# A graph network on one core: the five gather passes rebuilt on four row slots of 16 batches

## What is computed

```python
h = relu(layernorm(x))                     # before every layer
# layer 0, three times:
agg = segment_sum(h[src], dst, n)
h   = relu(concatenate([h, agg / (count + 1)]) @ W + b)
# layer 1: graph attention over the edges (and loops), then a feed-forward net
# layer 2:
aggr = segment_sum(relu(h[src] + edge_attr), dst, n)
z = (1 + eps) * h + aggr                   # then two matmuls with batch norms
# layer 3:
out = x + h + segment_sum(h[src] + edge_attr, dst, n)
```

## Time and profile before

| | us |
|---|---|
| three runs | 17120.43, 17063.85, 16991.23 (median 17063.85) |
| the profiled execution | 16898.69 |
| its span, first to last instruction | 16896.7 |

### The profile page before, as it was taken

How to read it: one execution, slowest core, us unless ns; L and a number is a source line. 1 busy time by engine, 2 the same in 40 slices (tenths; PEclk the granted TensorE clock), 3 DMA queues, 4 the chain that set the end, 5 groups by cost and what they waited for, 6 DMA issues and landing times. The chain is left out here.

```text
span 16896.7 us, 120575 instructions
## 1 busy us (share of the span) xinstructions
PE 6796.4 (40%) x30243; PEld 5870.2 (35%) x30244; DVE 3299.2 (20%) x6637; ACT 824.4 (5%) x1247; POOL 9578.3 (57%) x9860
## 2 busy tenths in 40 slices
PE   3444443333333444310000009996555555533333
PEld 2434333333333333200000008873555555333333
DVE  3222221111111222100000014444111112311111
ACT  1000000000000000000000000003000000200000
POOL 2666666666666666667777440001666664366666
PEclk8555555555555555555555555557555555655555
DMA  2111111111111222133333212222222222221212
GB/s 85 48 48 48 48 47 46 48 47 49 48 47 53 58 56 57 53 86 100 100 100 99 68 33 82 100 92 82 79 85 83 83 79 90 67 55 53 55 52 53
DMA packets 593156, 1124.64 MB, mean 67 GB/s; under 512 B 220826, under 2 KB 364385, under 8 KB 566579
## 3 DMA queue, kind: packets, MB, share of 16 engines
q0 software_dynamic: 307488, 624.42, 14.6%
q1 hardware_dynamic: 285622, 499.73, 8.8%
HBM read 904.32 MB, written 218.95 MB: 66 GB/s over the span
## 5 line engine op out<-in xcount | busy, mean ns | idle before, releaser
L680 POOL DMA_INDIRECT work<-rows_a,index x4704 | 4544.1, 966 | 2425.0 <-issue 1475.6
L751 PE MATMUL psum<-onehot,work 128*128 128x64 f32 x12544 | 2864.0, 416 | 3649.9 <-issue 1191.6
L680 POOL DMA_INDIRECT work<-rows_b,index x3136 | 3088.4, 985 | 1771.2 <-issue 1039.4
L751 PEld LDWEIGHTS psum<-onehot,work 128*128 128x128 f32 x12544 | 2721.0, 325 | 3797.5 <-issue 2795.1
L1191 POOL DMA_INDIRECT work<-attention_rows,index x1568 | 1608.7, 1026 | 610.6 <-issue 559.1
L751 PE MATMUL psum<-onehot,regionB 128*128 128x64 f32 x6272 | 1550.0, 417 | 720.8 <-issue 564.0
L751 PEld LDWEIGHTS psum<-onehot,regionB 128*128 128x128 f32 x6272 | 1438.7, 327 | 816.6 <-issue 789.8
L846 DVE TENSOR_TENSOR regionA<-regionA,psum 128x64 f32 x2352 | 508.7, 216 | 5116.3 <-remote 3598.3
L765 PE MATMUL psum<-onehot,regionB 128*4 128x64 f32 (+1 forms) x6272 | 1171.4, 358 | 467.2 <-issue 466.5
L765 PEld LDWEIGHTS psum<-onehot,regionB 128*4 128x4 f32 (+1 forms) x6272 | 1021.7, 224 | 516.9 <-issue 470.5
L182 POOL COPY work<-regionB 128x500 f32 (+1 forms) x75 | 45.3, 603 | 2030.6 <-DVE regionB L561 2030.6
(11 more groups left out here) (253 smaller groups left out, 4638.8 us busy)
## 6 DMA issues: line engine op xcount, KB each, us to landing
gathered_rows<-work SPq DMA_DIRECT2D x98, 1088.0 KB
work<-gathered_rows SPq DMA_DIRECT2D x98, 1088.0 KB, 4.9
regionB<-in_edge_attr SPq DMA_DIRECT2D x195, 512.0 KB
work<-rows_a,index POOLq DMA_INDIRECT x4704
work<-rows_b,index POOLq DMA_INDIRECT x3136
work<-attention_rows,index POOLq DMA_INDIRECT x1568
x_transposed<-regionA SPq DMA_DIRECT2D x75, 250.0 KB, 6.0
rows_a<-regionC SPq DMA_DIRECT2D x50, 250.0 KB
```

Of the source, the lines that this page charges most:

```text
L680: pool.indirect_dma_start(rows3[h][:, t, :], None, table, bass.IndirectOffsetOnAxis(ap=net.index[:, k, h * ST + t:h * ST + t + 1], axis=0) ...
L751: last = nc.tensor.matmul(bank_of(h, q, 0), msgs3[h][:, t, 0:D], onehot[:, h * ST + t, :], start=(k == 0), stop=(k == GT - 1))
```

## The change

`aggregate` is split: `attend` keeps the attention pass as it was, `gather_pass` is new and serves agg0, agg1, agg2, agg4 and agg5.
- Four row slots of 16 batches in region `B` (`SLOTS = 4`). The last two halves of the 98 are written out behind the loop of 24 rounds of four slots.
- One PSUM bank per slot. PE waits once per slot for `added` (the adds of the same slot's last use) and raises `summed` once per slot, after 16 batches.
- DVE casts 16 index columns per slot, behind the slot's adds, and raises `staged`; POOL waits for `staged` and `summed[s]`.
- Own features are no longer resident in `B`: n0 and n3 store `h` to HBM (`keep=True`), each chunk's own features are loaded two chunks ahead (`load_own`), and the Sage layers store theirs.
- The follow-up of a chunk runs in two parts: `vector` behind slot 3, `vector_late` and PE's part behind slot 1 of the next round.
- agg4 adds the attributes in place (`rows + attr` in `B`), ACT rectifies in place, attributes lie in `C` in four slots and no longer go through PE. `net.ES` is gone.
- agg5 loads the attributes itself and sums them on PE into the same group, 16 more matmuls per slot. `Finish` no longer loads the stored sum; its loads and stores are issued by ACT.

```diff
@@ gather_pass, was aggregate
-    S = 2 if attention or edges else 4
-    ST, SG = 2 * HALF // S, 2 * GPH // S
-    rows = [net.work[:, h * ST * XW:h * ST * XW + ST * width] for h in range(S)]
+    rows = [net.B[:, s * T:(s + 1) * T] for s in range(SLOTS)]
+    attr = [net.C[:, s * T:(s + 1) * T] for s in range(SLOTS)]
...
+    bank_of = lambda s, q, k=0: net.psum[:, s * 512 + k * GPH * W + q * W:s * 512 + k * GPH * W + (q + 1) * W]
...
+                def gather(j, s):
+                    pool.wait_ge(staged, r * (NHALF + 2) + j * SLOTS + s + 1)
+                    pool.wait_ge(summed[s], use(s, r, j) + 1)
+                    pool.sem_inc(allowed, 1)
+                    for t in range(HALF):
+                        pool.indirect_dma_start(
...
+                def load(j, s):
+                    if edges:
+                        sp.wait_ge(message[s], use(s, r, j) + 1)
+                    else:
+                        sp.wait_ge(summed[s], use(s, r, j) + 1)
...
+                def sums(j, s):
+                    pe.wait_ge(piled[s], built(r, j) + 1)
+                    if edges:
+                        pe.wait_ge(relued[s], use(s, r, j) + 1)
+                    else:
+                        pe.wait_ge(gathered[s], use(s, r, j) * 16 * HALF + 16 * HALF)
+                    if final:
+                        pe.wait_ge(attr_loaded[s], use(s, r, j) * 16 + 16)
+                    pe.wait_ge(added, half(r, j, s) * GPH + GPH)
+                    for q in range(GPH):
+                        for k in range(GT):
+                            t = q * GT + k
+                            last = nc.tensor.matmul(bank_of(s, q), rows3[s][:, t, :], onehot[s][:, t, :],
+                                                    start=(k == 0), stop=(k == GT - 1 and not final))
+                        for k in range(GT if final else 0):
+                            t = q * GT + k
+                            last = nc.tensor.matmul(bank_of(s, q), attr[s][:, t * D:(t + 1) * D], onehot[s][:, t, :],
+                                                    start=False, stop=(k == GT - 1))
...
+                    last.then_inc(summed[s], 1)
+                with pe.Fori(0, PAIRS) as j:
+                    for s in range(SLOTS):
+                        sums(j, s)
+                        if follow and s == 1:
+                            due_range(net, pe, j * 2 - 2, j * 2, lambda c: follow.tensor(pe, c))
...
+            if follow:
+                due_range(net, pe, NIT - 3, NIT - 1, lambda c: follow.tensor(pe, c))
+                due_range(net, pe, NIT - 1, None, lambda c: follow.tensor(pe, c))
...
+                def messages(s, j):
+                    dve.wait_ge(gathered[s], use(s, r, j) * 16 * HALF + 16 * HALF)
+                    dve.wait_ge(attr_loaded[s], use(s, r, j) * 16 + 16)
+                    nc.vector.tensor_tensor(rows[s], rows[s], attr[s], ALU.add).then_inc(message[s], 1)
...
+                with dve.Fori(0, PAIRS) as j:
+                    for s in range(SLOTS):
+                        add(j, s)
+                        n = dve.snap(j * SLOTS + (s + SLOTS))
+                        following = dve.snap(j + 1)
+                        stage(n, s)
+                        compare(n, s, following)
+                        if edges:
+                            messages((s + 2) % SLOTS, j if s < 2 else following)
+                        if follow and s == 1:
+                            due_range(net, dve, j * 2 - 2, j * 2, lambda c: follow.vector_late(dve, c))
+                    if follow:
+                        due_range(net, dve, j * 2, j * 2 + 2, lambda c: follow.vector(dve, c),
+                                  lambda: all_added(half(r, j, SLOTS) * GPH))
...
@@ gin_output
-            sp.dma_start(net.ES, Cc[:, 0:N]).then_inc(s["kept"], 16)
@@ new helper
+def load_own(net, sp, f, c):
+    if not isinstance(c, int):
+        sp.wait_ge(f.own_loaded, c * 16)
+    elif c:
+        sp.wait_ge(f.own_loaded, 16 * c)
+    sp.dma_start(own(net, c), net.HT[:, bass.ds(c * CH, CH)]).then_inc(f.own_loaded, 16)
```

571 lines of the change are left out of this document (314 added, 257 removed).

## The result

The kernel after takes 17,662.44 us (median of four, 17,583.29 to 17,703.93), the kernel before beside it 17,092.14 (16,991.23 to 17,220.62). The ratio is 1.0365, with a 95% interval of 1.0308 to 1.0421: slower by 3.7%, where the forecast was 15,780 and faster. (A ratio given with an interval is that of the executions in the faster state of the program, so it can differ from the quotient of the medians, which is 1.033 here.) The profiled execution took 17,583.29 us, its span is 17,581.1.

A forecast was written before the change was run, and what follows sets the result against it. POOL's indirect gathers bound the kernel, with some 1714 us of pauses from late PE signals. Five passes -1284, with +26 and -17, gave -1275: 15,624 us profiled, 15,780 with 1% carried; range 15,500 to 16,400.

The forecast's parts named there:

- 46 us are left for the signal: Ring of 4 x 16: 80 us until POOL's first slot wait, less 20 filling and 13.5 for landing, PE, adds, cast.
- 210 in all: POOL's pauses after the change: 30 us in agg0, agg1, agg5, 70 in agg2, 50 in agg4; bounds 0 and 1714.
- The term of agg5: Last pass: 16 more batches per slot on PE covered; attribute loads cost 55 ns x 1568 = 86 us.
- the rival to that term: agg5: descriptors wait for DVE, not traffic, so gathers stay at 959 ns, sum 86 us lower; no chance given.
- agg4 gained: Edge pass: four slots, attributes added in place, PE's work per slot halved; 2132 us forecast, -413.
- The tails: Ends of passes: three chunks left after the last gather instead of one; 122 us in Project, 48, 43, 20, 43 elsewhere.
- gin: This stage loses the 6.4 MB store ahead of its loads: about -17 us.
- n0 and n3: These stages now store h too: +13 us each, +26 together.
- the stage sums: Head, gathers, pauses and tail of agg0, agg1, agg2, agg4, agg5: 2081, 2038, 2162, 2132, 2129 us, together -1284.
- D: Gather passes: PE's signals come only when POOL pauses, Project's chain on top; pauses 1737 us, median 17,320; chance 0.04.
- B: Gather passes: POOL still stops 5.5 us once per ring, 135 us per pass, +465, total 16,250; chance 0.20.
- C: agg4 and agg5: traffic slows gathers to 1.383 us per DMA, +116 us each, total 16,010; chance 0.09.

The follow-up runs named there:

- a_attr_by_dve: Changed kernel with the last pass's attributes added to the rows by one VectorE instruction per slot, not 16 matmuls: ratio 1.0129 on chip D, 1.0070 on chip E.
- a_one_add: Changed kernel with VectorE adding a slot's four groups in one instruction at a fixed place, output wrong; about 15,230 us on chip B.
- a_half_one: Changed kernel with half of the sums' matmuls left out and one VectorE add per slot at a fixed place; about 15,280 us on chip B.
- a_third: The changed kernel as it is, run again on chip D: 15,291.95 us beside 15,162.70 for the kernel before.
- b_again: The kernel before, unchanged, profiled on chip C: 17,018 us, beside 17,339 for the changed kernel.

## Why the prediction was wrong

**The step that failed** is "So 46 us are left for the signal, against 25 as the longest seen", and the 30, 70, 50 and 30 us of pauses taken from it, "210 in all: near the lower end, as 25 is well under 46". Pauses came to 2,091 us. The step has two faults.

First, 25 us was neither the longest wait nor the delay. The earlier trace rows leave out agg4, where VectorE's waits in the kernel before reach 41.5 us (TensorE's own sums are a part of them):

```profile
DVE regionC L843 <- remote: 1094.9, 87, 41.5
```

And a wait begins only when VectorE gets there. Counted from the end of a group's last matmul to the start of its add (the ends are modelled, and VectorE's other work is in it), the kernel before has a median of 10.8 us in agg1 and 33.2 at most. The very sums of the earlier trace rows ended at 3026.36 and were added at 3051.85, 25.5 us later, behind a wait of 15.41. Nor do the next matmuls start at 3052.13; this row stands between the two that the earlier trace rows show:

```profile
3033.87 3.98 PE L751 MATMUL psum<-onehot,work 128*128 128x64 f32 x16 [5.80 <-DMA work<-rows_b,index]
```

So the 46 us were not far above what the trace held. In the kernel after the same count gives 58.7 us at most in agg1 and 61.0 in agg0, over the 46, and on chip D 0.7 in agg1.

Second, the step has the matmuls at full pace and only their signal late, by a length that a longer ring outlasts. What the runs showed in its place is that the streams themselves are slow beside the gathers (2.8 us a matmul instruction, 0.70 us a short VectorE one), so that they fall behind for as long as this lasts. "Why, I can't read; that it is late is what counts" was the sentence to stop at: the whole gain rested on how that delay goes with the ring. That the longer ring itself makes the backlog larger fits the longest wait, 20.9 us before and 82.7 after, and is not shown: the ring of 32 on a chip with slow streams is the run that is missing, and agg4 of the kernel before, with a ring of 32 batches, has 145 matmul instructions at 2.8 us where its agg1 has 8.

**The term of agg5** failed by the same cause. "16 more batches per slot on PE (14.6 of 20 us, covered)" is right where no stream is slow: on chip D the pass takes 2058 us with them. Where streams are slow they cost 264 to 301 us. The 86 us that I charged for the attribute traffic aren't there: on chip D agg5 has 982 ns a gather with the traffic and agg1 991 without. The Trainium skill, page SBUF — State Buffer, section "SBUF: two separate sides", by which descriptor writing waits for VectorE and not for traffic, was the rival to that term; these numbers agree with it in sign, and so do the 1034 ns of a_attr_by_dve. Its size doesn't follow from VectorE's work alone: on chip D agg0, with more of it than agg1, has 990 ns against 991, and on chip B agg1 has 974 in a_one_add and 994 in a_half_one, with the same adds.

**What came right.** agg4 gained, by 186 us and not 413: half its matmuls left. The tails are 47, 30, 105, 19 and 70 us against 48, 43, 122, 20 and 43 worked out. gin gave 14 (forecast 17), n0 and n3 15 and 11 (13 each). And where the streams aren't slow the stage sums are near: 2073, 2066, 2115, 2103, 2058 against 2081, 2038, 2162, 2132, 2129. That is in part luck, as terms cancel: in agg1 the gathers take 2031 us and not 1960, the pauses 0 and not 30, the tail 30 and not 43. The whole was forecast at 15,624 for the profiled execution, with gat_gather at 2190; chip D has 1995 there, which makes 15,429, and 15,292 was measured. But on such a chip the kernel before has none of the 1,714 us either, at least by its time: 16,899 less 1,714 less 195 is 14,990, and it takes 15,163. I had no profile of it there, so its stages on such a chip, and with them the 130 us between the two kernels, stay unread.

**The rivals.** D had the right outcome and nearest time (17,320), with half of the mechanism: it had signals come only in POOL's pauses. What happens is that TensorE's and VectorE's own instructions are held up as well. It had .04, and its condition, a delay of over 46 us, was the right one. B's pause per ring (24.5 a pass) is within a factor of two of the count (39, 28, 39, 21 and 47 pauses of over 2 us) and far from the length: 5.5 us priced, 8 to 13 in the median. C falls: the gathers of agg5 take 986 ns, not over 1.05 us.

**Why slower, and not even.** Where streams are slow no pass of any version here took under 2,266 us, so all stayed above the forecast's 2,040 to 2,160. agg5 got 3,136 more matmul instructions on TensorE, +389 to +413 us, which agg4 gives back only with 146 to 186; agg0 and agg1 lost 60 to 90 us each. Of that last piece 25 to 38 us are the longer gathers of agg1 (979 ns against 955 to 963) and 6 to 20 the tail; the rest is longer pauses, and which part of the new order makes them was not settled.

## What to carry to other kernels

Before pricing a stall that the trace doesn't name ("remote", "issue"), ask whether it grows with the load: a delay may be outlasted by a deeper buffer, a backlog is not. Measure a late signal from the end of the work to its use; the waiting engine's own wait shows only a part of it. Take a second profile on a second chip before building on a wait, since here the kernel before took 15,160 us on two of the chips and 17,000 on the others. Where streams of instructions are slow beside indirect DMAs, work moved from many small instructions to one large one gained in one pass (a_attr_by_dve, -264 to -301 us), and where they aren't it lost there (+76). Halving the matmuls of the kernel before gained in one pass of five, so try it before counting on it.

## What the runs showed of the hardware

Beside indirect DMAs the other engines' streams were slow on chips A, C, E and on that of the first profiles: 2.8 us per matmul instruction, 0.70 us per short VectorE instruction, and 1.38 us per gather in gat_gather, with TensorE idle. On chips B and D the same programs showed 1.263 us per gather in gat_gather (1980 us from first to last) and nothing slow.

The slow instructions of both engines keep one step. In agg1 of the kernel after, TensorE's matmuls start 0.70, 1.4, 2.1, 2.8 or 3.5 us behind the one before (67, 49, 73, 201 and 14 of them, to 0.05 us), and VectorE's short instructions last 0.70 or 1.4 us (494 and 23). In the same pass of a_third there are 1 and 6 such matmuls and no such VectorE instruction.

The two kinds of chip differ in one more thing. Here are the gathers in the list of DMA issues (count, then the median us from issue to landing), first of after, then of a_third:

```profile
regionB<-rows_a,index POOLq DMA_INDIRECT x4704
...
work<-attention_rows,index POOLq DMA_INDIRECT x1568
```

```profile
regionB<-rows_a,index POOLq DMA_INDIRECT x4704, 2.5
regionB<-rows_b,index POOLq DMA_INDIRECT x3136, 2.5
work<-attention_rows,index POOLq DMA_INDIRECT x1568, 2.5
```

Where streams are slow the column is empty: most landings have no record. A pass makes 1568 x 16 = 25,088 increments from its gathers. Between first and last gather of agg1 the trace of a_third holds 25,944 records of landings by all DMAs, that of after 4,246, b_again 5,431. In all twenty traces the two go together: whole records where the streams are quick, lost records where they are slow. That, and the common step of 0.70 us, speak for one outlet through which the records of all engines and queues leave, too narrow on some chips for 16 increments in 1.3 us plus the instructions. The Trainium skill, page NOTIFIC — the notification-queue block, section "Overflow: three behaviours, one of which stalls the engine", says that a full queue may drop new records while the block's inner pipeline always holds its producers back; the traces would fit both halves, the four in five landing records that are missing and the streams held up, but none shows whether a queue was full. It isn't proved: every execution timed here also carries a profile's records, so whether the slow streams are there without recording was not tried and can't be told. Nor can what makes one chip quick, since a chip and its surroundings were never varied apart.
